# Summing two key tiles together in every fourth step of an attention kernel, with the projections dealt out over the other twelve steps

## What is computed

```python
xn = layernorm(x)                                  # x: 8 batches x 1024 tokens x 512
q, k, v = heads(xn @ Wq.T), heads(xn @ Wk.T), heads(xn @ Wv.T)   # 16 heads of 32
diff = maximum(|q|^2 + |k|^2 - 2 q.k, 0)
denom = maximum((1 - |q|^2) * (1 - |k|^2), 1e-6)
c = maximum(1 + 2 * diff / denom, 1)
attn = softmax(-arccosh(c))                        # over the 1024 keys
out = x + (attn @ v) @ Wo.T + (xn @ quantised(kernel) + bias + xn @ a @ b)
```

## Time and profile before

| | |
|---|---|
| time, median of 3 runs | 2383.63 us (2381.73 to 2385.03) |
| the profiled execution | 2382.27 us, its span in the trace 2380.5 us |
| PE busy | 2267.3 us, 95% |
| DVE busy | 2090.4 us, 88% |
| ACT busy | 2089.2 us, 88% |
| POOL busy | 256.1 us, 11% |
| granted TensorE clock, mean | 0.992 |

### The profile page before, as it was taken

One profiled execution on the slowest core, in us unless ns is written; L12 is line 12 of the kernel. 1 busy time (PEld: TensorE's weight loads), 2 busy tenths in 40 slices (PEclk: granted clock), 3 DMA queues, 4 the chain that ended last, 5 costly groups with the idle time before them and its releaser, 6 DMA issues.

```text
span 2380.5 us, 45534 instructions
## 1 busy us (share of the span) xinstructions
PE 2267.3 (95%) x17416; PEld 812.5 (34%) x17416; DVE 2090.4 (88%) x2794; ACT 2089.2 (88%) x1909; POOL 256.1 (11%) x193
## 2 busy tenths in 40 slices
PE   6999999999999999999999999999999999988877
PEld 2433333333333333333333333333333333322222
DVE  7779988899988898988889988889998888888887
ACT  4379999999999999998998999999999999999993
POOL 0101110110111111011111011011101111100012
PEclk9999999999999999999999999999999999999999
DMA  4343343543545443454424454353354543334442
GB/s 155 116 140 98 103 104 96 141 109 103 145 129 147 108 122 105 126 141 134 129 84 138 110 147 128 114 144 106 107 136 134 141 120 108 101 112 97 113 114 86
DMA packets 355428, 285.04 MB, mean 120 GB/s; under 512 B 81132, under 2 KB 294252, under 8 KB 355208
## 3 DMA queue, kind: packets, MB, share of 16 engines
q1 hardware_dynamic: 355208, 282.10, 42.8%
HBM read 159.77 MB, written 121.36 MB: 118 GB/s over the span
## 4 chain that ended last, share of the span: by engine, by line
PE 56%; DVE 17%; issue 12%; ACT 11%; DMA 2%; SPq 1%; ACTq 0%; DVEq 0%; POOL 0%; POOLq 0%
PE pM L305 20%; PE pU L225 12%; PE pO L237 12%; PE pZ L253 7%; DVE root L859 6%; ACT root L522 5%; ACT root L528 5%; DVE root L864 3%; DVE stats L671 1%; DVE shares L786 1%; DMA z_d<-z_s 1%; DMA zc<-z_d 1%; PE pM L295 1%; PE pM L278 1%; DVE ah L787 1%
## 5 line engine op out<-in xcount | busy, mean ns | idle before, releaser
L522 ACT ACTIVATE root<-pU 128x1024 f32<-128x1024 f32 x1008 | 1016.5, 1026 | 83.8 <-PE pU L225 80.2
L528 ACT ACTIVATE root<-root 128x2048 f32<-128x2048 f32 x512 | 981.0, 1916 | 95.1 <-DVE root L859 94.5
L859 DVE TENSOR_SCALAR root<-root 128x2048 f32<-128x2048 f32 (+1 forms) x512 | 662.5, 1294 | 59.1 <-ACT root L522 54.0
L225 PE MATMUL pU<-QS,KS 100*128 100x512 f16 x2048 | 614.9, 384 | 67.5 <-ACT root L522 58.6
L864 DVE TENSOR_TENSOR root<-root 128x2048 f32<-128x2048 f32 x256 | 585.3, 2286 | 28.7 <-PE pO L237 25.7
L237 PE MATMUL pO<-root,VX 128*32 128x512 f32 x4096 | 550.0, 607 | 3.4 <-DVE o_s L849 2.0
L225 PEld LDWEIGHTS pU<-QS,KS 100*128 100x128 f16 x2048 | 145.3, 98 | 606.0 <-issue 281.6
L253 PE MATMUL pZ<-root,ones 128*32 128x512 f32 x2048 | 272.5, 601 | 2.7 <-DVE root L864 2.7
L1013 POOL TENSOR_TENSOR sqr<-qk 128x512 f32<-128x512 f32 x112 | 152.0, 1357 | 1060.7 <-ACT qk L549 917.4
L305 PE MATMUL pM<-Wqh,xT 128*128 128x512 f16 x480 | 162.8, 383 | 2.5 <-DVE f_o L778 1.5
L305 PE MATMUL pM<-Wvh,xT 128*128 128x512 f16 x480 | 161.9, 379 | 0.6 <-DVE Wvl L650 0.6
(11 more groups left out here) (228 smaller groups left out, 2181.3 us busy)
## 6 DMA issues: line engine op xcount, KB each, us to landing
v_d<-v_o SPq DMA_DIRECT2D x64, 264.0 KB, 2.1
k_d<-kx SPq DMA_DIRECT2D x64, 264.0 KB, 2.1
KT<-k_d SPq DMA_DIRECT2D x64, 264.0 KB
VX<-v_d SPq DMA_DIRECT2D x64, 264.0 KB
xts<-in_x SPq DMA_DIRECT2D x32, 512.0 KB, 4.2
res_d<-f_o SPq DMA_DIRECT2D x64, 256.0 KB, 4.0
QS<-qh_d SPq DMA_DIRECT2D x128, 128.0 KB
KS<-kh_d SPq DMA_DIRECT2D x128, 128.0 KB
```

What stands on the lines that cost most here:

```text
L225: mm = pe.matmul(pU[:, col:col + HALF], KS[i][:, h, j * P:(j + 1) * P], QS[i][:, h, half * HALF:(half + 1) * HALF], start=True, stop=True)
L522: act.activation(root[:, q % RING, cols], pU[:, cols], ACT.Square).then_inc(squared, 1)
L528: act.activation(root[:, q % RING, :], root[:, q % RING, :], ACT.Sqrt).then_inc(rooted, 1)
L859: v.tensor_scalar(root[:, q % RING, cols], root[:, q % RING, cols], CS * CS, CS * CS, ALU.max, ALU.subtract).then_inc(clamped, 1)
```

## The change

On TensorE the sums move to the steps with s % 4 == 3, right behind `distances(s + 1)` and ahead of `behind(p, k)`: two `sum_v`, one `sum_one`, and in even periods at k = 11 both parts of the key sums. Nothing else is left in steps 3, 7, 11 and 15; projections, transposes and the output product are dealt out anew over the other twelve. VectorE's and SyncE's lists are shifted to match, the squares that VectorE takes are those at k = 7 and 15. ScalarE's list, RING and the arithmetic stay as they are. The core of the diff:

```diff
-        by_vector = [16 * p + k for p in range(LATE, PERIODS) for k in (5, 13)]
+        by_vector = [16 * p + k for p in range(LATE, PERIODS) for k in (7, 15)]
...
-                    if k in (2, 3):
-                        project(n, "k", 1, 6 * k - 12, 6 * k - 6)
-                    if k == 4 and n + 1 < NT:
-                        pe.wait_ge(taken["q"], n + 1)
-                        transpose_x(n + 1, 0)
-                    if k in (5, 6):
-                        project(n, "v", 1, 6 * k - 30, 6 * k - 24)
+                    if k in (2, 4):
+                        project(n, "k", 1, 3 * k - 6, 3 * k)
+                    if k == 5:
+                        if n + 1 < NT:
+                            pe.wait_ge(taken["q"], n + 1)
+                            transpose_x(n + 1, 0)
+                        pe.wait_ge(taken["k"], n + 1)
+                        project(n, "v", 1, 0, 4)
+                    if k == 6:
+                        project(n, "v", 1, 4, 10)
+                    if k == 8:
+                        project(n, "v", 1, 10, 12)
...
-                    if even and k in (7, 8):
-                        output(o, 0, 6 * k - 42, 6 * k - 36)
-                    elif not even and k in (7, 8, 9):
-                        output(o, 0, 4 * k - 28, 4 * k - 24)
...
-                if even and k in (9, 11):
-                    key_sums(p, k // 2 - 4)
+                        output(o, 0, 0, 4)
+                    if k == 9:
+                        output(o, 0, 4, 10)
+                    if k == 10:
+                        output(o, 0, 10, 12)
...
+                if s % 4 == 3:
+
+                    if s >= 7:
+                        sum_v((s - 7) // 2)
+                        sum_v((s - 5) // 2)
+                    if s >= 9:
+                        sum_one((s - 9) // 2)
+                    if p % 2 == 0 and k == 11:
+                        keys(p)
                 behind(p, k)
-                if s % 2 and 0 <= (s - 5) // 2 < QUADS:
-                    sum_v((s - 5) // 2)
-                if s % 4 == 1 and 0 <= (s - 7) // 2 < QUADS:
-                    sum_one((s - 7) // 2)
...
-                    if k == 5 and n + 1 < NT:
-                        split_x(n + 1, 0)
                     if k == 6:
+                        if n + 1 < NT:
+                            split_x(n + 1, 0)
                         norm(n, 1)
+                    if k == 7:
                         factors(n)
                         scale_qk(n)
...
-                if s % 4 == 3 and 0 <= (s - 5) // 2 < QUADS:
-                    add_pair((s - 5) // 2)
+                if s % 4 == 1 and s >= 9:
+                    add_pair((s - 7) // 2)
```

More of the change, by code:

```diff
@@ L369, in behind @@
                             pe.wait_ge(taken["o"], o)
-                    if even and k in (7, 8):
-                        output(o, 0, 6 * k - 42, 6 * k - 36)
-                    elif not even and k in (7, 8, 9):
-                        output(o, 0, 4 * k - 28, 4 * k - 24)
[L374 to L379, removed]
-                if even and k in (9, 11):
-                    key_sums(p, k // 2 - 4)
+                        output(o, 0, 0, 4)
[3 more added lines that the diff above has]
+                        output(o, 0, 10, 12)
                 if p == PERIODS - 1:
-                    if k == 10:
+                    if k == 12:
                         pe.wait_ge(kv_taken, PERIODS // 2)
                         pe.wait_ge(three_divided, 1)
-                    if k == 12:
+                        output_last(60, pM[1], 0, 9)
+                    if k == 13:
                         pe.wait_ge(taken["o"], o + 1)
[L388 to L391, removed]
+                    if k in (13, 14):
+                        output_last(61, pM[0], 5 * k - 65, 4 * k - 47)
                 if n < NT:
                     if k == 10:
-                        if not even:
-                            pe.wait_ge(taken["v"], n + 1)
-                        elif o >= 0:
+                        pe.wait_ge(taken["v"], n + 1)
+                        transpose_feat(n, 0, 1)
+                    if k == 12 and not even:
+                        if o >= 0:
+                            pe.wait_ge(taken["o"], o + 1)
+                        else:
+                            pe.wait_ge(x_split, n + 2)
+                        transpose_feat(n, 1, 0)
+                    if even and k == 12:
+                        if o >= 0:
                             pe.wait_ge(taken["o"], o + 1)
@@ L399, in behind @@
                             pe.wait_ge(x_split, n + 2)
-                        transpose_feat(n, 0, 0 if even else 1)
-                    if k == 12:
+                    if not even and k == 12:
                         pe.wait_ge(feat_split[0], n + 1)
@@ L409, in behind, with keys @@
                         transpose_feat(n, 1, 1)
[L410 to L415, removed]
+            def keys(p):
+                n = p + LEAD
+                if n < NT:
+                    pe.wait_ge(feat_split[0], n + 1)
+                else:
+                    pe.wait_ge(kv_taken, p // 2)
+                pe.wait_ge(stack_loaded[p // 2 % 2][1], (p // 4 + 1) * STACK)
+                key_sums(p, 0)
+                key_sums(p, 1)
             pe.wait_ge(small_loaded, 3 * 16)
@@ L894, in behind @@
                 if o >= 0:
-                    if even and k == 1:
+                    if even and k == 3:
                         divide(o)
-                    if k == (9 if even else 10):
+                    if k == 10:
                         take_o(o, 0)
-                if not even and k == 10 and o % TPB == TPB - 1 and -1 <= o < NT - 9:
+                if not even and k == 12 and o % TPB == TPB - 1 and -1 <= o < NT - 9:
                     invert_z((o + 1) // TPB)
-                if p == PERIODS - 2 and k == 10:
+                if p == PERIODS - 2 and k == 12:
                     invert_z(NB - 2)
@@ L913, in behind @@
                     if k == 11:
-                        split_feat(n, 0, 0 if even else 1)
-                    if k == 12 and not even:
+                        split_feat(n, 0, 1)
+                    if k == 13 and not even:
                         split_feat(n, 1, 0)
@@ L979, in vector_program @@
                     square(s)
[L980 removed]
+                if k == 8 and p > LATE:
                     take_one_sums(p - 1)
                 behind(p, k)
[L983 to L984 removed]
+                if s % 4 == 1 and s >= 9:
+                    add_pair((s - 7) // 2)
+            add_pair(QUADS - 3)
             clamp(QUADS - 1)
@@ L1204, in behind @@
                     store_v(n)
-                if k == (9 if p < PERIODS - 1 else 7) and p:
+                if k == 9 and p:
                     store_att(p - 1)
@@ L1211, in behind @@
                     store_aug(n)
-                if k == (10 if even else 11) and o >= 0:
+                if k == 11 and o >= 0:
                     store_out(o)
@@ L1215, in behind @@
                     load_raw(o + 1, (o + 1) // TPB)
-                if k == 12 and last_of_block:
+                if k == 13 and last_of_block:
                     store_rz((o + 1) // TPB, (o + 1) // TPB)
@@ L1223, in behind @@
                     load_z(NB - 1, NB - 2, p, H - G4)
-                if p == PERIODS - 2 and k == 12:
+                if p == PERIODS - 2 and k == 13:
                     store_rz(NB - 1, NB - 2, H - G4)
@@ L1238, in behind @@
                         load_res(57)
-                if k == 13 and not even and n < NT:
+                if k == 14 and not even and n < NT:
                     store_feat(n)
```

12 lines of the change are left out of this document (5 added, 7 removed).

## The result

The changed kernel takes 2550.78 us (median of 4 runs, 2548.07 to 2554.0) against 2382.72 before: 1.0704 times as long, 95% interval 1.0686 to 1.0723. The forecast was 2482 with a range up to 2525. The sign and the loop through the ring came out; the size did not, by 69 us, because the cost of TensorE's clock had been left out of the sum.

The account below looks back on a forecast made before the run. TensorE bound the middle stage, ScalarE close behind; a loop through the ring would replace it. First stage +12.7, middle +57.1, period 55 +4.6, last +21.4, opening and end +2: +98 on 2382.3, 2480; median 2482 us, range 2430 to 2525.

Parts of the forecast that it names:

- The sign: Whole kernel: the change makes it slower, chance 0.88, against 0.09 for faster and 0.03 for the same.
- the loop through the ring: ScalarE's first square waits for a group's sums, the next group for the third square: at least 8.06 us, plus evictions.
- TensorE's saving: Eight groups of sums become four: 0.76 us a period, 49 us over 64; rival that it comes through, 2335 us, chance 0.09.
- the cycle k = 3 to 7: Four steps of a period between group openings: predicted to take 10.38 us, with TensorE waiting 1.55.
- k = 7 to 11: Next four steps of a period: chain 8.30 plus 0.46 for pZ and 0.49 for v, 9.25 us.
- 2.4 at k = 3 to 7: Microseconds that evictions, with the wait, were said to add to that cycle; used as argument against the saving coming through.
- The eviction of k: ScalarE, k = 3 to 7: it waits for its product, which ends a step later, and starts at 5.55, not 4.61.
- I cost them at nothing: VectorE's clamps, pair sums, splits, norm and factors at their new places: all end before they are needed, no time added.
- I leave it out of the sum: TensorE's clock falling in the last stage: 2.5 us a group, 28 groups, +70 us as upper end, not summed.
- a rival of 0.15: The clock falls too, in most last-stage groups or in the middle: 2517 to 2552 us for the last stage alone, chance 0.15.
- 92.5% busy before: First stage: TensorE had full clock at 92.5% busy, so the clock was expected to fall only in the last stage.
- opening and end: Start and finish of the kernel, outside the stages: +2 us together.

Follow-up runs that it names:

- combo_fill: Changed kernel with sum of ones first, k's eviction and GpSimd's addition later, VectorE's split before output eviction in even periods, and unread matmuls added; 2388.36 us, 1.0024 times before.
- tight_before: Kernel before the change, with only the sum of ones moved two steps later; 2456.99 us, 1.0311 times before.
- tight_ring7: tight_before with a ring of seven quads instead of six, f's output not right; 2374.33 us, 0.9958 times before.
- k_late: Changed kernel with ScalarE's eviction of k behind the square of step 5 instead of step 4; 2520.37 us, 1.0579 times before.
- pool_later: Changed kernel with GpSimd's bias addition waiting for the split of q's features instead of their transposes; 2540.07 us, 1.0652 times before.
- fill: Changed kernel with four more unread f16 matmuls in each step that lost its work, in the first and last stages; 2492.26 us, 1.045 times before.

## Why the prediction was wrong in size

- *TensorE's saving.* Never the bound of a period in the changed kernel, whose TensorE is busy 93% of the middle stage. No run measures the term of 0.76 us a period by itself; combo_fill's odd periods, 33.92 us against 34.3 to 35.0 in most of those before, are in keeping with it.
- *The ring and the loop.* Right, and shown by tight_before with tight_ring7. Odd periods at 36.18 us against 36.17, the cycle k = 3 to 7 at 10.26 against 10.38, k = 7 to 11 at 9.31 against 9.25. The total is closer than its parts: k = 15 to 3 takes 8.45 us (8.48) and k = 11 to 15 8.15 (8.06), and the four errors cancel. The prediction's "2.4 at k = 3 to 7", by which it argued against the saving, is 1.98 by its own figures (10.38 - 8.40).
- *The eviction of k* adds what was worked out (k_late, 0.83 us).
- *"I cost them at nothing": VectorE.* This step failed, by a modest sum. Even periods take 37.29 us, not 36.75, or 12.9 us over the middle stage. Most of it, 0.48 us, is a clamp that now meets GpSimd's addition (pool_later). I had the split of q's features end before the key sums need it, and it ends 0.30 us after.
- *"I leave it out of the sum": the clock.* This is the step that made the prediction wrong. The prediction had worked out a wait of 2.3 us ahead of each group of the last stage (2.10 measured), and it had a row of a sum at 1.2 GHz behind a wait of 1.86 us; yet it put the term at nothing in the sum and kept it as a rival of 0.15. Holding the clock up gave back 58.5 us (fill), 39.4 of 60 us in the profiled executions in the last stage and 12.6 in the first. Its price for a slow group, 2.5 us, was near what such groups cost (2.99 us in the cycle shown, 2.0 on average over the 20). The measured 2550.8 lies inside the 2517 to 2552 that the rival gave for the last stage alone, and that is in part luck: the last stage exceeds the forecast by 45.5 us, and 15.3 us in the first stage and 12.9 in the middle make up most of the rest. For the first stage I had read 92.5% busy before as proof that waits cost no clock there. In the new order the steps k = 8 to 10 have little left in that stage, which has no output products, so the waits lie together in front of one group (0.21, 1.29 and 1.66 us in the rows above), and the stage's clock fell to 0.93.
- *The rest.* 2492 with the clock held, less 13 for even periods, leaves about 2479, so the other terms of 2482 hold in sum. Stage by stage fill is 2.7 (first), 13.3 (middle) and 6.1 us (last) above the forecast; its opening and end together are 6 us shorter than before, where 2 longer had been allowed, and that offsets the last stage.
- *What was not in it.* The second loop through pU; it doesn't change the sum, since the ring's is longer, but it sets what opening the ring can give.

Of the remaining 2.29 us between odd and even periods of combo_fill, 0.89 lie in the cycle k = 7 to 11 (9.71 against 8.82 us) and 1.41 in k = 11 to 15 (9.09 against 7.68), where the key sums lengthen the group by 1.09. In the former, two roots of ScalarE wait 0.81 and 0.45 us for VectorE's clamps in an even period, and none does in the same cycle of an odd one; one of these clamps takes 2.06 us beside GpSimd's squares of qk. Still open is what taking those waits away would give: no run does it. A version with a ring of seven quads and all weights kept was not tried; tight_ring7 is 10 us faster than before, but with f's low weights given up for the room.

## What to carry to other kernels

Before gathering work into bursts on the busiest engine, write down for each buffer that the burst releases which instruction waits for it, and follow that one back to what opens the next burst; the sum around this loop, not the engine's busy time, is the new pace. The last reader of a ring belongs first in the burst. If the loop leaves TensorE idle ahead of a dense group, put the group at half clock into the sum from the start; here 20 of the 28 groups of the last stage ran slow, and the wait behind a slow group was no longer than behind a fast one.

## What the runs showed of the hardware that was not expected

- Four unread f16 matmuls of 512 columns in each empty step (0.87 us a step) took 58.5 us off the changed kernel and added 14 us to the one before. The middle stage, with waits of 1.30 and 0.91 us ahead of two groups of each period, kept a granted clock of 1.00. The last stage, with waits of 2.10 us ahead of three of four groups in most periods, had 0.85. One group behind a wait of 2.11 us (opening at 2241.56) ran at full clock all the same.
- A VectorE clamp of 128x2048 f32 takes 2.32 us when GpSimd's 1.26 us addition starts beside it, and 1.16 to 1.23 when nothing of GpSimd runs beside it: here 1.10 of GpSimd's 1.26 us are added. All 49 clamps of this shape that take over 1.35 us in the changed kernel overlap an instruction of GpSimd, and so do all 58 in the kernel before, where most meet its squares of qk. Others overlap one and are not slower.
